# The first tiles of a query stage: a mean over three products instead of four, two tiles interleaved, and an earlier rounding

## What is computed

```python
def _layernorm(x, axis=-1, eps=1e-05):
    m = jnp.mean(x, axis=axis, keepdims=True)
    v = jnp.var(x, axis=axis, keepdims=True)
    return (x - m) / jnp.sqrt(v + eps)
...
q = rms_norm(linear(x, q_w, q_b), norm_q_w).reshape(B, L, NH, HD)
k = rms_norm(linear(ctx_txt, k_w, k_b), norm_k_w).reshape(B, -1, NH, HD)
v = linear(ctx_txt, v_w, v_b).reshape(B, -1, NH, HD)
...
out = (txt_x + img_x).reshape(B, L, DIM)
return linear(out, o_w, o_b)
...
x = x + _L0_xattn_ref(_layernorm(x, axis=-1), ctx_2048, ...)
x = x + _L0_ffn_ref(_layernorm(x, axis=-1), ...)
```

## Time and profile before

| | us |
|---|---|
| median of 3 runs | 1509.78 |
| lowest, highest | 1508.43, 1510.69 |
| the profiled execution, in all | 1507.41 |
| its span | 1505.7 |

### The profile page before, as it was taken

One profiled execution on the slowest core, in us unless ns is written; L12 is line 12 of the kernel. 1 busy time (PEld: TensorE's weight loads), 2 busy tenths in 40 slices (PEclk: granted clock), 3 DMA queues, 4 the chain that ended last, 5 costly groups with the idle time before them and its releaser, 6 DMA issues.

```text
span 1505.7 us, 41153 instructions
## 1 busy us (share of the span) xinstructions
PE 1479.5 (98%) x16188; PEld 1163.7 (77%) x16188; DVE 1184.7 (79%) x1917; ACT 720.5 (48%) x1489; POOL 681.7 (45%) x761
## 2 busy tenths in 40 slices
PE   8999999999999999999999999999999999999997
PEld 6877777777777777777777777777776887777997
DVE  6865788878888888888878888878887586564986
ACT  5874444444444444444444444444445225665431
POOL 3543344444444444444444444444445582214852
PEclk9999999999999999999999999999999999999999
DMA  7962121211121211121211111211134521310000
GB/s 256 339 217 78 35 65 53 82 51 57 51 63 51 83 51 57 51 63 51 83 51 56 52 63 51 82 52 53 55 101 155 186 113 57 140 57 29 1 1 25
DMA packets 70343, 121.04 MB, mean 80 GB/s; under 512 B 21984, under 2 KB 36672, under 8 KB 68752
## 3 DMA queue, kind: packets, MB, share of 16 engines
q1 hardware_dynamic: 69456, 117.54, 23.7%
q0 software_dynamic: 832, 2.75, 0.6%
HBM read 89.93 MB, written 30.34 MB: 80 GB/s over the span
## 4 chain that ended last, share of the span: by engine, by line
PE 91%; DVE 5%; ACT 2%; issue 1%; POOL 1%; DMA 0%; DVEq 0%; ACTq 0%; SPq 0%; POOLq 0%
PE ps L1621 22%; PE ps L1623 19%; PE ps L1622 19%; PE ps L1777 10%; PE ps L1740 5%; PE ps L1713 3%; PE ps L1684 2%; PE ps L1986 2%; PE ps L2003 2%; PE ps L1746 2%; PE ps L1995 1%; DVE rec L1224 1%; PE ps L1664 1%; PE ps L1749 1%; DMA q_all<-q_dram 0%
## 5 line engine op out<-in xcount | busy, mean ns | idle before, releaser
L1224 DVE RECIPROCAL rec<-ps 128x224 f32<-128x224 f32 x128 | 198.1, 1548 | 3.0 <-PE ps L1777 3.0
L565 POOL TENSOR_TENSOR ctx_lo<-ctx_raw,ctx_hi 128x512 fp32r<-128x512 f32 (+1 forms) x93 | 118.8, 1277 | 119.8 <-ACT ctx_hi L809 119.8
L599 POOL TENSOR_TENSOR prob_img<-prob 128x448 f32<-128x448 f32 x93 | 106.8, 1149 | 115.0 <-ACT prob L877 115.0
L1207 DVE TENSOR_REDUCE top<-ps 112x4 f32<-112x1028 f32 x128 | 156.1, 1220 | 0.0
L1206 DVE TENSOR_REDUCE top<-ps 112x4 f32<-112x472 f32 x128 | 83.1, 649 | 37.1 <-PE ps L1713 36.1
L1621 PE MATMUL ps<-w_k_img_hi,ctx_hi 128*128 128x512 f32 x256 | 110.2, 431 | 0.0
L1621 PE MATMUL ps<-w_v_img_hi,ctx_hi 128*128 128x512 f32 x256 | 107.1, 418 | 0.0
L1740 PE MATMUL ps<-q_all,k_all 32*128 32x112 f32 (+1 forms) x3072 | 105.5, 268 | 0.0
L1192 DVE SCALAR_TENSOR_TENSOR proj<-proj,rstd,w_img 128x512 f32<-128x512 f32 x64 | 48.0, 751 | 67.7 <-POOL rstd L592 67.7
L1623 PE MATMUL ps<-w_v_img_hi,ctx_lo 128*128 128x512 f32 x256 | 100.8, 394 | 0.0
L1623 PE MATMUL ps<-w_k_img_hi,ctx_lo 128*128 128x512 f32 x256 | 100.7, 394 | 0.0
(11 more groups left out here) (364 smaller groups left out, 4366.9 us busy)
## 6 DMA issues: line engine op xcount, KB each, us to landing
ctx_raw<-in_ctx_dram SPq DMA_DIRECT2D x32, 748.0 KB, 4.6
xh_dram<-xh SPq DMA_DIRECT2D x32, 448.0 KB
xc<-in_xT_dram SPq DMA_DIRECT2D x28, 256.0 KB, 4.2
q_dram<-q_turned SPq DMA_DIRECT2D x28, 256.0 KB, 4.4
q_all<-q_dram SPq DMA_DIRECT2D x32, 224.0 KB, 3.1
out_dram<-out_sb SPq DMA_DIRECT2D x32, 224.0 KB, 2.3
xh<-in_x_dram SPq DMA_DIRECT2D x31, 224.0 KB, 3.0
proj<-in_x_dram SPq DMA_DIRECT2D x21, 256.0 KB, 5.0
```

The lines of the kernel that those rows point to most:

```text
L565: nc.gpsimd.tensor_tensor(ctx_lo[:, :, cols], ctx_raw[:, :, cols], ctx_hi[:, :, cols].bitcast(F32), ALU.subtract).then_inc(ctx_lo_done, 1)
L599: nc.gpsimd.tensor_tensor(prob_img[:, g % 2], image[:, 0, :], image[:, 1, :], ALU.add).then_inc(img_summed, 1)
L1207: nc.vector.tensor_reduce(rows[:, :, 2 * g + 1], ps[0:L, 2:6, TAIL:CTX], AX.X, ALU.max).then_inc(s_done, 1)
L1224: nc.vector.reciprocal(rec[:], values_bank(g)[:, 2:4]).then_inc(norm_step, 1)
```

## The change

It does five things.

- The mean is a sum over four quarters of the weights. PE now multiplies two quarters singly and the sum of the other two, which DVE adds up first (`pair_sum`, in the buffer `q_turned1`). `centred` counts this sum too, so `query_piece` waits for one more.
- Tile 0's product goes to bank 4 (`q_bank`). The wait of `queries(2)` for `qp_done` of tile 0 stands as it was.
- `first_queries` now runs tiles 0 and 1: the four high passes of tile 1 stand between the two pairs of `w_q_lo` passes of tile 0.
- ACT rounds tile 3, tile 4 and tile 5 earlier in its order and tile 6 a little later, and `x_hi(1)` waits only for `xc1`. From tile 7 on ACT's order is as before.
- DVE and POOL take `ln1` and `invert_spread` of tiles 1 to 6 later, and SP issues `xc1` ahead of `xa0`, `q_bias` earlier, and `xa1`, `xc3` and `xa3` after `xc1` has landed.

The diff, cut to what decides (the order of DVE, ACT and POOL stands above):

```diff
+        pair_sum = q_turned[1][:].rearrange("p c l -> p (c l)")
+        def q_bank(t_):
+            return ps[:, t_ % 2 if t_ else 4, :]
@@ sync
                 sp.wait_ge(piece_loaded[1], 16)
+                load_xc(1)
                 load_xa(0)
-                load_x(1)
+                load_x(2)
+                sp.dma_start(q_bias[:], t["q_b"].partition_broadcast(P)).then_inc(q_bias_loaded, 16)
+                sp.wait_ge(x_loaded[1], 16)
+                load_xa(1)
+                load_x(3)
                 sp.dma_start(pick_rows[:], t["pick_rows"]).then_inc(pick_loaded, 16)
@@ scalar
-                act.wait_ge(x_loaded[t_ % 4], 32 * (t_ // 4) + 32 if t_ else 16)
+                act.wait_ge(x_loaded[t_ % 4], 32 * (t_ // 4) + 32 if t_ > 1 else 16)
-                    act.wait_ge(centred, c + 1)
+                    act.wait_ge(centred, c + 2)
+                x_hi(1)
                 act.wait_ge(consts_ready, 1)
-                for k in range(NT + 1):
-                    if k + 1 < NT:
+                x_hi(2)
+                q_squares(0)
+                x_hi(3)
+                q_scale(0)
+                x_hi(4)
+                q_squares(1)
+                q_scale(1)
+                x_hi(5)
+                for k in range(3, NT + 1):
+                    if 5 < k < NT - 1:
                         x_hi(k + 1)
+                    if k == 4:
+                        x_hi(6)
@@ vector
                 x_rest(0)
+                dve.wait_ge(piece_loaded[1], 16)
+                nc.vector.tensor_tensor(pair_sum, stage[:, 1, 0:D], stage[:, 1, D:2 * D], ALU.add).then_inc(centred, 1)
                 for c in range(KC):
                     centre(c)
@@ tensor
+                pe.wait_ge(centred, 1)
+                nc.tensor.matmul(ps[:, 6, :], mean_w, pair_sum, start=False, stop=True).then_inc(mean_full, 1)
@@ first_queries
+                pe.wait_ge(piece_lo, 1)
+                query_pass(0, xT_hi, w_lo, (0, 1))
+                pe.wait_ge(xT_hi_done, 2)
+                query_pass(1, xT_hi, w_hi, range(KC), start=True)
+                pe.wait_ge(piece_lo, 2)
+                query_pass(0, xT_hi, w_lo, (2, 3), stop=True).then_inc(qp_full, 1)
+                pe.wait_ge(xT_lo_done, 2)
+                query_pass(1, xT_lo, w_hi, range(KC))
+                query_pass(1, xT_hi, w_lo, range(KC), stop=True).then_inc(qp_full, 1)
```

More of the change, by code:

```diff
@@ L1292, in pre @@
                 add_q_bias(0)
+                ln1(1)
+                x_rest(3)
                 ln1(2)
-                for k in range(1, NT):
-                    if 1 < k < NT - 1:
-                        x_rest(k + 1)
-                    if k + 2 < NT:
+                add_q_bias(1)
+                add_q_bias(2)
+                x_rest(4)
+                ln1(3)
+                ln1(4)
+                for k in range(3, NT):
+                    if 3 < k < NT - 1:
+                        x_rest(k + 1)
+                    if k == 4:
+                        ln1(5)
+                    if k == 5:
+                        ln1(6)
+                    if 4 < k < NT - 2:
                         ln1(k + 2)
@@ L1631, in weight_means @@
             def weight_means():
[L1632 to L1636 removed]
+                pe.wait_ge(piece_loaded[0], 16)
+                for c in range(2):
+                    nc.tensor.matmul(ps[:, 6, :], mean_w, stage[:, 0, c * D:(c + 1) * D], start=c == 0, stop=False)
+                pe.wait_ge(centred, 1)
+                nc.tensor.matmul(ps[:, 6, :], mean_w, pair_sum, start=False, stop=True).then_inc(mean_full, 1)
             def queries(t_, half):
@@ L1642, in queries @@
                         pe.wait_ge(qp_done, t_ - 1)
-                made = project((bank0, bank1)[t_ % 2], xT_hi[t_ % 2], xT_lo[t_ % 2], slice(0, P), "q", range(2 * half, 2 * half + 2))
+                made = project(q_bank(t_), xT_hi[t_ % 2], xT_lo[t_ % 2], slice(0, P), "q", range(2 * half, 2 * half + 2))
                 if half:
@@ L1647, in first_queries, with query_pass @@
             def first_queries():
+                def query_pass(t_, x_part, w_part, chunks, start=False, stop=False):
+                    for kc in chunks:
+                        made = nc.tensor.matmul(q_bank(t_), x_part[t_][:, kc, :], w_part["q"][:, kc, :], start=start and kc == 0,
+                                                stop=stop and kc == KC - 1)
+                    return made
                 pe.wait_ge(xT_lo_done, 1)
@@ L1786, in pre @@
                 first_queries()
-                for k in range(1, NT):
+                for k in range(2, NT):
                     queries(k, 0)
```

41 lines of the change are left out of this document (15 added, 26 removed).

## The result

The change makes the kernel slower. The changed kernel's median is 1513.92 us (1511.73 to 1514.74, 16 runs) beside 1509.60 (1507.67 to 1512.38, 16 runs) of the kernel before: a ratio of 1.0025, with a 95% interval of 1.0018 to 1.0031. In a second comparison it is 1.0019 (1.0010 to 1.0029). The forecast was 1508.0 and a gain of 1.8 us; what came is a loss of some 3 to 4 us. The profiled execution took 1514.28 us for a span of 1512.5, against 1507.41 for 1505.7.

What follows compares the result with a forecast made beforehand. PE was taken to bound the kernel, with 91% of the chain and no idle from 24 to 104 us. Mean product 0.84 + order 1.0 - 0 for later tiles = 1.8 us gained, so 1508.0 us; range 1506.1 to 1510.2.

Steps and rivals of the forecast that it cites:

- Every microsecond by which S3 moves is a microsecond of the whole: Query stage: an earlier tile 3 start shortens the whole run equally, if the engines around PE keep up later.
- S3: Start of tile 3 in PE's query stage: forecast 20.9 instead of 22.73, 1.8 us earlier.
- it costs nothing: Mean product: DVE's added 128x512 sum ends near 7.4, before the fifth pass needs it at about 8.3.
- The mean product: Ahead of the centring: dropping one fp32 product of two passes saves 2 x 0.42 = 0.84 us; centring at 9.40.
- Tiles 0 and 1: Query stage start: first pass 10.89 instead of 11.73; four tile 1 passes fill PE's 0.40 us gap; worth nothing alone.
- Tile 2: Query stage: PE still waits for DVE's bias of tile 0; start 17.4 instead of 18.59, after 0.4 us idle.
- Tile 3: Query stage: rounding ahead of ACT's scaling; start 20.9, ended by DVE's bias 1, 1.8 us earlier.
- 1.0 of the order: Tile 3's start: the part of its 1.8 us gain credited to the new order of work, 1.0 us.
- Tiles 4 to 8: Rest of the query stage: whether tile 3's gain is kept; loss taken as 0, with 0.3 as other end.
- S7: Start of tile 7 in PE's query stage: forecast 33.95, with DVE's rest ending just in time at 33.9.
- B: Rival, chance 0.17: tile 5's load or ACT's work ahead of tile 7 comes late; only 0.9 is left, 1508.9.
- C: Rival, chance 0.06: transfers set the query stage, later load +0.9, 1510.7; in "C + 8.0", start of DVE's first centring.

## Why the prediction was wrong

**"Every microsecond by which S3 moves is a microsecond of the whole": this is the step that failed.** It was applied to work that moves, and I never asked what a change does to code that stays. Adding one DVE instruction ahead of the loop costs 0.37 us in the first of its 28 passes and some 0.10 in each other, 3.1 us in all, more than the whole of the forecast gain. The sum was priced "it costs nothing", and as work that was nearly right. As one instruction more ahead of a loop it brought that loss, and so does a fill of one column. No rival named it. Nothing in the trace of before could have given its size, but the place was to be had: the chain of a loop of 32 batches, with a wait of an engine for its own last instruction in it, was left out of the reading since the diff doesn't touch it. The chance of 0.03 for slower was too small for that reason alone.

**The mean product, 0.84.** Two steps of 0.42, and that was right. It is hard to see, since C differs between executions of one kernel by 0.9 us. PE's weight loads in two profiles of the changed kernel, in which one step is 0.43 and the other 0.85:

```profile
6.66 0.19 PEld L1666 LDWEIGHTS ps<-prob,q_turned 128*128 128x128 f32 x1 [0.28 <-issue]
7.09 0.19 PEld L1666 LDWEIGHTS ps<-prob,q_turned 128*128 128x128 f32 x1 [0.24 <-issue]
7.71 0.43 PEld L1668 LDWEIGHTS ps<-q_turned 128*128 128x128 f32 x2 [0.43 <-DVE q_turned L1304]
```

```profile
6.91 0.33 PEld L1666 LDWEIGHTS ps<-prob,q_turned 128*128 128x128 f32 x1 [0.52 <-issue]
7.76 0.23 PEld L1666 LDWEIGHTS ps<-prob,q_turned 128*128 128x128 f32 x1 [0.52 <-issue]
```

The step is 0.85 up to the trace's first record of a whole clock and 0.43 behind it, in every profile. So C follows the start of that record, and profiles with equal starts have to be compared:

| first record of a whole clock at | C, four products | C, sum on DVE |
|---|---|---|
| 5.45 and 5.57 | 9.40 | 8.95 |
| 6.37 and 6.41 | 9.84 | 9.01 |
| 7.16 and 7.06 | 10.24 | 9.33 |

That is 0.83 in the second row and 0.9 in the third. The plain means, 10.02 over the seven profiles with four products and 9.50 over the nine with the sum on DVE, differ by 0.5 only, mostly since the clock started 0.5 later on average in the nine. Of the 1.23 us between the two profiles of the result, some 0.8 are the change's and 0.4 are luck: 6.41 for 7.16. In the first fence PE waits for the sum, at 7.71, 0.2 later than the step of 0.42 would have it, and in the first row of the table the gain is only 0.45: where the clock starts early the cover for the sum is gone. The prediction had the cover too large: the pass that needs the sum is the fifth, whose weights were loaded at 7.90 in the kernel before, not near 8.3. The sum on POOL takes 1.26 us and PE's load waits 1.37 for it where 0.24 is usual, so that version gives a part of it back.

**Tiles 0 and 1.** Right: the first pass is at 10.51 for C = 9.01, so C + 1.50 as predicted (10.9 for 9.40), and the four passes of tile 1 fill the gap.

**Tile 2.** Predicted at C + 8.0, ended by the bias. It was the bias that ended it (1.10 idle, `q_row`), but at C + 8.78. The term that was mis-sized is "from that start to the end of POOL's `tile_rstd` it took 1.90": it took 2.47 (14.28 to 16.75), since POOL's step now starts together with DVE's `x_rest(2)`. In the earlier trace rows it had started 0.29 us ahead of that operation, at 16.83:

```profile
17.12 0.66 DVE L1170 TENSOR_TENSOR xT_lo<-xc,xT_hi 128x512 fp32r<-128x512 f32 x1
```

With the sum on POOL, which starts POOL 0.06 ahead of DVE, tile 2 is at C + 8.14. That the left-in wait for `qp_done` takes the worth of the own bank was right.

**Tile 3.** Predicted at C + 11.5: "1.0 of the order". Measured C + 12.25, so 0.24; with POOL's step at 0.58 it is C + 11.62, so 0.87. The chain was read rightly (bias 0, `ln1`, bias 1 end it, not `xT_lo`), and the missing part was POOL's 0.56 and some 0.1 that was not traced further.

**Tiles 4 to 8.** "Just in time for S7. I take 0 for it": it was 0.6. ACT's row went as written up to the scaling, and there it waited 0.33 for POOL's `tile_inv`, which stood behind the variance and inverse root of another tile:

```profile
31.33 1.06 ACT L916 ACTIVATE w_k_hi<-prob 128x1024 fp32r<-128x1024 f32 x1
32.71 0.72 ACT L837 ACTIVATE q_row<-q_row,tile_inv 128x512 f32<-128x512 f32 x1 [0.33 <-POOL tile_inv L582]
33.34 0.61 ACT L827 ACTIVATE xT_hi<-xc 128x512 fp32r<-128x512 f32 x1
```

I had counted ACT's own work and not whom ACT waits for. PE's step there is 3.83 instead of 3.23. The loads were in time, and the rest of the stage went as predicted: from 1.47 at S3, 0.60 was lost at tile 7, and 0.90 was left at the first key pass (102.95 for 103.85) with the rounding. Counted from C, that pass is at 93.94 for 93.61: the new order gains 0.24 at S3, loses 0.60 at tile 7, and so costs some 0.33 by the end of the stage. What the head can keep of the change is 0.84 - 0.33, about 0.5 us, and not 1.8.

**The rivals.** B had the right mechanism for tile 7. C, which held the whole chance for slower, was not it: from 40 to 60 us the changed kernel moved 369 GB/s, more than the 356 of the earlier trace rows, and PE was busy 20.00 of 20 us. The Trainium skill's figure of about 358 GB/s (DMA: Bandwidth & Descriptors, Where 436 GB/s comes from) as one core's share of HBM was thus not a limit for this stretch. Only this core ran the kernel, and some of the loads there repeat one row for every partition, so whether more than that share crossed HBM is not shown.

```profile
40.00:60.00 20.00, 20.00 (x101) 1.00 1.06 369
```

**The bridge to the median.** The profile of before lay 2.4 us below the median, and I carried that over as it was. It is now known what is in it: passes of the last stage at either pace, 2.5 us, and the clock after batch 0, 1.5 us, neither of which the profile of before had. The changed kernel's profile had both, and so 6.8 us of difference between two profiles stand for 3 to 4 us between medians. The medians differ by about the loop's 3.1 less the head's 0.5, plus the clock's 1.5 in those executions where it falls; with the wait filled, and so without that term, the changed kernel's ratio is 1.0013, or 2.0 us (0.6 to 3.3). The range, by its own words 1506.0 to 1510.0 and not 1506.1 to 1510.2, misses 1513.92 either way.

What stays open: by what rule DVE's 0.10 comes at one count and moves at another; what sets the start of the clock's record; and what sets the pace of the last stage.

## What to carry to other kernels

An instruction added ahead of a loop can change the loop's own pace, and a loop that runs 30 times turns 0.1 us into more than the gain that is being worked for; so where a change touches only a head, compare the steady step of the loop before and after first, and if it moved, try the same change with one idle instruction more or fewer on that engine. A small GpSimd step on the critical path is to be priced with what VectorE starts beside it. And a small gain is only seen against several profiles of each kernel, matched by what differs by chance: here 0.9 us at the centring and 2.5 us in the last stage between executions of one kernel, and 1.5 us after batch 0 in code that is the same in all.

## What the runs showed of the hardware

- The idle time between two VectorE instructions in a loop depended on how many VectorE instructions stand ahead of it in the program: 0.16 us with as many as in the kernel before and with 2, 4, 9 and 17 more, and 0.26 us with one more, in every profile, with six kernels at the first count and five at the last. The first pass through the loop waited 0.53, and the copies of the same code outside the loop stayed at 0.14 to 0.16. With 9 more another pair was 0.05 us further apart.
- A 128x1 GpSimd operation of 0.58 us took 1.12 to 1.14 us when a 128x512 VectorE `tensor_tensor` started with it or up to 0.02 us ahead, and 0.58 when it started 0.06 or 0.29 us ahead itself.
- Passes of 128x448 at the full granted clock ran 0.2027 or 0.2067 us apart for the whole last stage, in two executions of the same program.
- After 2.2 to 2.4 us in which PE did nothing, its granted clock fell to half for some 3 us in ten profiles (1.5 us lost), and not in eight others with the same wait. All ten falls came 146.8 us after the first record of a whole clock. Twenty-four transposes in that wait kept it whole in both programs that had them.
- The passes of the fp32 products at the start of the program followed each other at 0.85 us up to the first record of a whole clock and at 0.43 behind it; that record started anywhere from 5.4 to 8.6 us, and with it moved all that follows by up to 0.9 us.
